# A two-layer graph network on one core: bf16 pieces by TensorE, later zero fills, words moved into layer 0, and another order of layer 1's tiles

## What is computed

```
h = relu(layernorm(x))
x = x + relu(h @ W_self + mean over edges(h[src]) @ W_neigh + b)           # layer 0
h = relu(layernorm(x))
e = sigmoid(relu([h[src], h[dst]] @ We1 + be1) @ We2 + be2)                 # one gate per edge
m = e * h[src];  messages = [max over edges(m), sum over edges(m)]
x = x + relu([messages, h] @ Wn1 + bn1) @ Wn2 + bn2 + h                     # layer 1
```

## Time and profile before

| | |
|---|---|
| median of 3 runs | 5438.78 us (5437.1 to 5440.79) |
| the profiled execution | 5435.6 us, span of its instructions 5433.9 us |
| busy DVE, POOL, ACT, PE | 4035.2, 3687.3, 2774.4, 2013.7 us |
| search | 0 to 179 us |
| sorting, ranks, words | 179 to 455 us |
| layer 0 | 455 to 2170 us |
| the rest of the early gathers | to 2435 us |
| layer 1 | 2435 to 5296 us |
| output scatters | to 5434 us |

### The profile page before, as it was taken

The page is one execution under the profiler, slowest core; times in us unless marked ns, Lnnn a source line. Parts: engine busy times, 40 slices in busy tenths (PEclk is TensorE's granted clock), DMA queues, the critical chain, the costliest instruction groups (busy, mean ns, idle before and its releaser), DMA issues.

```text
span 5433.9 us, 105141 instructions
## 1 busy us (share of the span) xinstructions
PE 2013.7 (37%) x18241; PEld 1777.4 (33%) x18241; DVE 4035.2 (74%) x8508; ACT 2774.4 (51%) x7285; POOL 3687.3 (68%) x3830
## 2 busy tenths in 40 slices
PE   0005899999999998000111111111111111111110
PEld 0004888888888888000000000101011111111110
DVE  6788788888888886006777778878888888887770
ACT  7304777887888886003444444444445444544440
POOL 5545216777777777767777777777777777766547
PEclk9999999999999999555555555555555555555555
DMA  7610315555555555554434444444444444443440
GB/s 212 166 24 27 41 52 173 160 160 158 163 160 160 158 163 167 158 156 101 124 113 124 124 122 125 124 133 126 132 133 135 133 142 136 142 134 118 123 98 24
DMA packets 491280, 696.11 MB, mean 128 GB/s; under 512 B 249885, under 2 KB 339843, under 8 KB 491163
## 3 DMA queue, kind: packets, MB, share of 16 engines
q0 software_dynamic: 181472, 381.28, 26.1%
q1 hardware_dynamic: 228085, 172.05, 10.3%
q10 hardware_dynamic: 81638, 141.95, 7.8%
HBM read 513.68 MB, written 163.18 MB: 125 GB/s over the span
## 4 chain that ended last, share of the span: by engine, by line
PE 22%; issue 20%; POOL 19%; DVE 17%; DMA 8%; ACT 7%; ACTq 4%; DVEq 3%; POOLq 0%; SPq 0%
POOL counts_f L580 13%; PE ps_acc L1867 10%; PE ps L1859 9%; DMA counts_f<-early_rows 5%; POOL extra_f L580 4%; DVE act_w L1450 4%; ACT counts_f L1627 3%; DMA counts_f<-hA_table,stage 2%; DVE pre L1444 2%; DVE run_max L1467 2%; ACT msg L1726 1%; DVE z L1456 1%; POOL out_dram L727 1%; ACTq L1726 1%; DVE pre L1059 1%
## 5 line engine op out<-in xcount | busy, mean ns | idle before, releaser
L580 POOL DMA_INDIRECT counts_f<-hA_table,stage x2144 | 2070.9, 966 | 794.3 <-issue 632.1
L1627 ACT ACTIVATE counts_f<-ps 128x784 bf16<-128x784 f32 x1568 | 1269.3, 823 | 468.6 <-PE ps L1859 385.7
L1444 DVE TENSOR_TENSOR pre<-counts_f,ps 128x512 f32 (+1 forms) x862 | 588.6, 683 | 825.2 <-SPq L897 316.9
L580 POOL DMA_INDIRECT extra_f<-hA_table,estage x984 | 932.1, 947 | 314.4 <-issue 290.4
L1726 ACT ACTIVATE msg<-counts_f,gate (+1 forms) x3448 | 921.5, 337 | 315.9 <-ACT gate L1721 293.8
L1867 PE MATMUL ps_acc<-pieces_f,counts_f 128*128 128x192 bf16 x9604 | 1021.3, 247 | 2.4 <-issue 2.4
L1867 PEld LDWEIGHTS ps_acc<-pieces_f,counts_f 128*128 128x128 bf16 x9604 | 885.7, 138 | 3.3 <-issue 2.8
L1859 PE MATMUL ps<-hot 128*128 128x196 bf16 x6272 | 820.6, 253 | 127.0 <-ACT counts_f L1627 106.5
L1938 PE MATMUL ps_acc<-ident,h_tile 128*64 128x128 f32 x98 | 38.6, 394 | 2210.3 <-DVE cat L1503 2210.3
L1721 ACT ACTIVATE gate<-z,be_col (+1 forms) x862 | 256.2, 297 | 1165.1 <-DVE z L1456 820.5
L1938 PEld LDWEIGHTS ps_acc<-ident,h_tile 128*64 128x64 f32 x98 | 12.6, 129 | 2226.4 <-issue 2226.4
(11 more groups left out here) (231 smaller groups left out, 2853.5 us busy)
## 6 DMA issues: line engine op xcount, KB each, us to landing
early_rows<-extra_f SPq DMA_DIRECT2D x294, 384.0 KB
counts_f<-early_rows ACTq DMA_DIRECT2D x98, 1152.0 KB
counts_f<-hA_table,stage POOLq DMA_INDIRECT x2144
counts_f<-counts_f SPq DMA_DIRECT2D x67, 288.0 KB
extra_f<-hA_table,estage POOLq DMA_INDIRECT x984
own<-own_rows ACTq DMA_DIRECT2D x98, 130.0 KB
hA_table<-node ACTq DMA_DIRECT2D x98, 96.0 KB
ranked_rows<-zeros SPq DMA_DIRECT2D x1, 3724.0 KB, 50.4
```

Source lines behind the costliest of these rows:

```text
L580: return pool.indirect_dma_start(to, None, table, bass.IndirectOffsetOnAxis(ap=idx, axis=axis))
L1444: v.tensor_tensor(pre[:, :, :], rows[:, :, D:WROW], ps_b[:, bass.ds(i & 1, 1), :].to_broadcast([P, SLOTS, H]), ALU.add).then_inc(s_pre, 1)
L1627: act.activation(counts[:, c, nodes, :].rearrange("p (b h) t -> p b (h t)", h=2), ps_pairs[g & 1][:, :].rearrange("p (b w) -> p b w", b=BA ...
```

## The change

1. ACT's wait for its input goes into the loop of the search. The first search step counts a pair of columns, then takes the rows of that pair, and stages them, instead of waiting for all ten columns first.
2. The two zero fills are issued after the twelfth of the fourteen sorted stores.
3. The second and third pieces are made by PE and ACT in 14 groups of 7 tiles: PE puts features minus first piece (identity and negative identity) in PSUM, ACT copies it to bf16; then the same with both pieces taken off. POOL's four subtractions and ACT's two large copies go. The negative identity `minus_b` is a new constant.
4. The sum over 64 bins becomes six additions that halve the array.
5. The words for degrees over 64 (`node_deg`) are made right after `s_thr`; the others (`late_words`) between phase(3, 1) and phase(4, 0) of layer 0, and a new semaphore `s_places` holds back POOL (before the early gathers), SP (before the loads of late rows) and ACT (before layer 1).
6. A tile of rank t goes to place min(2t, 2T-1-2t): heaviest, lightest, second heaviest, second lightest and so on. `tile_rank` is made to fit (8 small instructions for one), and two instructions move each node's place.

```diff
-            pool.wait_ge(s_first, 2 * TITER)
-            for h in range(2):
-                half = slice(h * (T // 2), (h + 1) * (T // 2))
-                pool.tensor_tensor(x_nodes[:, half, :], h_nodes[:, half, :], pieces[:, half, 0:D], ALU.subtract
-                                   ).then_inc(s_rest, 1)
...
-                pool.tensor_tensor(pieces[:, half, 2 * D:3 * D], x_nodes[:, half, :], pieces[:, half, D:2 * D],
-                                   ALU.subtract).then_inc(s_piece, 1)
...
             pool.wait_ge(s_row, 16)
+            pool.wait_ge(s_places, 1)
...
-            sp.wait_ge(s_start, 1)
+            with in_one_block(sp, 0, TITER - 1) as it:
+                store_sorted(it)
             sp.dma_start(extra_rows.rearrange("(t p) d -> p t d", p=P),
...
             sp.dma_start(ranked_rows.rearrange("(t p) w -> p t w", p=P),
...
+            store_sorted(TITER - 1)
...
             sp.wait_ge(s_recw, 16 * T)
+            sp.wait_ge(s_places, 1)
...
+            st.link(v.tensor_scalar(tile_rank[:, :], half_f, -2.0, float(T - 1), ALU.mult, ALU.add))
+            st.link(v.scalar_tensor_tensor(out=tile_rank[:, :], in0=tile_rank[:, :], scalar=odd_f, in1=half_f,
+                                           op0=ALU.mult, op1=ALU.add))
+            st.done(v.tensor_scalar(tile_rank[:, :], tile_rank[:, :], float(P), 1.0, ALU.mult, ALU.add))
...
-            search_step(0)
+            for a in range(PARTS):
+                at = slice(PASS + a * PCOLS, PASS + (a + 1) * PCOLS)
+                count(0, a)
+                rows_of(at, PASS + (a + 1) * PCOLS)
+                stage_rows(at, a)
...
+            rounded_up(node_deg[:, :], RUN, crow[:, 2, :], 1)
+            st.link(v.tensor_scalar(crow[:, 2, :], crow[:, 2, :], -1.0, 1.0, ALU.add, ALU.max))
+            word_sums(crow[:, 2, :], 8)
...
-            v.wait_ge(s_piece, 2)
+            v.wait_ge(s_piece, 2 * TITER)
...
-            st.link(v.tensor_reduce(cols2[:, :], order.rearrange("p b t -> p t b"), AX.X, ALU.add))
+            half = BINS // 2
+            while half > 1:
+                at = order_flat[:, 0:half * T]
+                st.link(v.tensor_tensor(at, at, order_flat[:, half * T:2 * half * T], ALU.add))
+                half //= 2
+            st.link(v.tensor_tensor(cols2[:, :], order_flat[:, 0:T], order_flat[:, T:2 * T], ALU.add))
...
+            st.link(v.tensor_scalar(cols[:, :], cols3[:, :], -2.0, float(2 * T - 1), ALU.mult, ALU.add))
+            st.link(v.scalar_tensor_tensor(out=cols3[:, :], in0=cols3[:, :], scalar=2.0, in1=cols[:, :],
+                                           op0=ALU.mult, op1=ALU.min))
...
+            phase(3, 0)
+            phase(3, 1)
+            late_words()
+            phase(4, 0)
+            phase(4, 1)
...
-            act.wait_ge(s_q, 2)
             with in_one_block(act, 0, SITER) as it:
+                act.wait_ge(s_q, 2)
...
+            def second(g):
+                act.wait_ge(s_rest, max(1, 2 * g))
+                act.activation(tiles_of(g, 1), rest_in(g), ACT.Copy).then_inc(s_sec, 1)
...
+            act.wait_ge(s_places, 1)
...
+            def rest(g):
...
+                pe.matmul(bank, ident[:, :], h_nodes[:, at, :].rearrange("p t d -> p (t d)"), start=True, stop=False)
+                pe.matmul(bank, minus_b[:, :], pieces[:, at, 0:D], start=False, stop=True).then_inc(s_rest, 1)
```

More of the change, by code:

```diff
@@ L404, in gnn_kernel @@
         s_ctl = sem("s_ctl")
+        s_places = sem("s_places")
         s_tidx = sem("s_tidx")
@@ L749, in _, with store_sorted @@
             sp.dma_start(flat_src[E:E + SRC_PAD].unsqueeze(0), src_tail[0:1, :]).then_inc(s_tab, 16)
-            sp.wait_ge(s_start, 1)
+            sorted_by_tile = sorted_rows.rearrange("(t p) w -> p t w", p=P)
+            def store_sorted(it):
+                for h in range(2):
+                    wait_alone(sp, s_srt, 4 * it + 2 * h + 2)
+                    tiles_at = bass.ds(it * (2 * THALF) + h * THALF, THALF)
+                    sp.dma_start(sorted_by_tile[:, tiles_at, :], rows_sb[:, tiles_at, :]).then_inc(s_srtw[h], 16)
+            with in_one_block(sp, 0, TITER - 1) as it:
+                store_sorted(it)
             sp.dma_start(extra_rows.rearrange("(t p) d -> p t d", p=P),
@@ L1361, in _ @@
             phase(2, 1)
-            for q in range(3, 5):
-                phase(q, 0)
-                phase(q, 1)
+            phase(3, 0)
[3 more added lines that the diff above has]
+            phase(4, 1)
             first = st.now()
@@ L1612, in _, with rest_in, tiles_of, third @@
                 act.dma_start(h0_by_tile[:, tiles_at, :], h_nodes[:, tiles_at, :]).then_inc(s_h0w, 16)
-            for h in range(2):
-                half = slice(h * (T // 2), (h + 1) * (T // 2))
-                act.wait_ge(s_rest, h + 1)
-                act.activation(pieces[:, half, D:2 * D], x_nodes[:, half, :], ACT.Copy).then_inc(s_sec, 1)
+            def rest_in(g):
+                return ps_4[:, (g & 1) * BANK:(g & 1) * BANK + THALF * D].rearrange("p (t d) -> p t d", d=D)
+            def tiles_of(g, k):
+                return pieces[:, g * THALF:(g + 1) * THALF, k * D:(k + 1) * D]
+            def second(g):
+                act.wait_ge(s_rest, max(1, 2 * g))
+                act.activation(tiles_of(g, 1), rest_in(g), ACT.Copy).then_inc(s_sec, 1)
+            def third(g):
+                act.wait_ge(s_rest, min(2 * g + 3, 4 * TITER))
+                act.activation(tiles_of(g, 2), rest_in(g), ACT.Copy).then_inc(s_piece, 1)
+            second(0)
+            for g in range(1, 2 * TITER):
+                second(g)
+                third(g - 1)
+            third(2 * TITER - 1)
             act.wait_ge(s_w, W_DMAS)
@@ L1833, in _, with rest_of_rest @@
             pe.matmul(ps_y[:, 2 * D:2 * D + 1], ones[0:1, 0:P], thr[0:1, 0:1], start=True, stop=True).then_inc(s_thrb, 1)
+            def rest(g):
+                if g >= 2:
+                    pe.wait_ge(s_piece, g - 1)
+                bank = ps_4[:, (g & 1) * BANK:(g & 1) * BANK + THALF * D]
+                at = slice(g * THALF, (g + 1) * THALF)
+                pe.matmul(bank, ident[:, :], h_nodes[:, at, :].rearrange("p t d -> p (t d)"), start=True, stop=False)
+                pe.matmul(bank, minus_b[:, :], pieces[:, at, 0:D], start=False, stop=True).then_inc(s_rest, 1)
+            def rest_of_rest(g):
+                pe.wait_ge(s_sec, g + 1)
+                bank = ps_4[:, (g & 1) * BANK:(g & 1) * BANK + THALF * D]
+                at = slice(g * THALF, (g + 1) * THALF)
+                pe.matmul(bank, ident[:, :], h_nodes[:, at, :].rearrange("p t d -> p (t d)"), start=True, stop=False)
+                pe.matmul(bank, minus_b[:, :], pieces[:, at, 0:D], start=False, stop=False)
+                pe.matmul(bank, minus_b[:, :], pieces[:, at, D:2 * D], start=False, stop=True).then_inc(s_rest, 1)
+            pe.wait_ge(s_first, 2 * TITER)
+            rest(0)
+            for g in range(1, 2 * TITER):
+                rest(g)
+                rest_of_rest(g - 1)
+            rest_of_rest(2 * TITER - 1)
             pe.wait_ge(s_bins, 1)
```

91 lines of the change are left out of this document (48 added, 43 removed).

## The result

The changed kernel takes **5262.13 us** (median of 4 runs, 5257.23 to 5262.5), the kernel before 5437.94 beside it on the same chip; the ratio is **0.9675 (95%: 0.9659 to 0.9692)**. Forecast were 5268, between 5238 and 5325. The profiled execution took 5262.5 (span 5260.8), 173.1 us of span less than before.

A forecast was written before the change was run, and what follows sets the result against it. Layer 1 was taken as bound by POOL in heavy tiles and DVE's early-row loads in light ones, the front by DVE. 48.4 us ahead plus 121 in layer 1, 169 off 5435.6, plus 3.2 gave 5268, range 5238 to 5325.

The forecast's parts named there:

- What bounds layer 1: Layer 1: POOL bounds the heavy tiles; in light ones POOL waits for DVE, held by early-row loads 24.4 us apart.
- the 121: Layer 1: with tiles alternated POOL never waits, so its gathers take 2722 us instead of 2843, 121 less.
- Search: Search ahead of layer 0: ACT's wait inside its loop and counts first save 9 us, bounds 0 and 10.
- Zero fills: Sort stage: without early fills, 3 us less at the run gathers and 3 at DVE's loop entry, -6.
- Pieces: Ahead of layer 0: DVE's 25.05 us instruction falls to 0.63 once POOL's subtractions are gone, -24.4 us.
- Sum over bins: Ahead of layer 0: six additions replace the 11.85 us sum over bins, two added instructions cost 0.5; -4.2 us.
- Words: 13.8 us leave the path ahead of layer 0; 36 instructions inside it cost PE 9; net -4.8.
- Scatters and what lies behind: After layer 1's gathers: the 98 scatters go on at 1.29 us and end with the span, unchanged.
- (a): Layer 1: ring too small or early loads later, only part of the stalls go; gain 50 there, 5341; chance 8%.
- (b): Layer 1: alternation does nothing, each tile still goes by its slower engine; only 48 us gained, 5391; chance 4%.
- (c): Ahead of and in layer 0: loop-entry gaps stay, PE loses 12; 33 of 48 us left, 5285; chance 8%.
- (d): Layer 1: POOL's gathers stretch beside busier DVE; gain gone at 0.079 us more each, 5512 at mean 1.08; chance 2%.

The follow-up runs named there:

- e9: e1 with one more DVE maximum (128x1024 fp32, about 1.2 us) in each layer 1 tile but the first and last: 5411.06 us, ratio 0.9956.
- e1: The changed kernel with layer 1's tiles back in order of load, all else kept: 5384.18 us, ratio 0.9903.
- e2: The kernel before with only the alternating order of tiles added: 5309.78 us, ratio 0.9772.
- e7: The changed kernel with ACT's wait for the nodes' ids ahead of its search loop again: 5267.91 us, ratio 0.9687.
- e6: The changed kernel with the two zero fills issued early again, at s_start, ahead of the sorted stores: 5266.47 us, ratio 0.9682.
- e3: The changed kernel with the pieces made as before, by POOL's four subtractions and ACT's two large copies, without PE: 5288.9 us, ratio 0.9729.
- e4: The changed kernel with the late words in one block ahead of layer 0, right before s_ctl: 5264.85 us, ratio 0.9682.
- e10: The changed kernel with layer 1's messages in PSUM instead of SBUF: 5232.23 us, ratio 0.9623.

## Why the prediction was right, step by step

**What bounds layer 1.** Right. POOL bounded it wherever it didn't wait, the light tiles went by their load's round, and DVE was the bound of neither half: e9 shows that 1.2 us more of it per tile don't lengthen a light tile. The pace of 1.27 us a gather, on which the 121 stood, measured 1.269 (2720.0 us for 2143 steps). Measured gain 123.1, and 122 to 125 in e1 and e2. Of the 123, 113 are POOL's long gaps and 10 are gathers less often stretched (mean 966 before, 961 after); the prediction had no term for the second. Two small slips in its working: light tiles have up to 9 chunks, by its own 21 columns, where it says 8; and its range doesn't follow from the cases named for it. A pace of 1.255 with the words free gives about 5228, not 5238, and a gain of 90 with 30 ahead gives 5319, not 5325. The result lies within either.

**Search** (-9): measured -7.4 at `s_start`, of which the wait's place 6.4 (e7, 177.81 against 171.36). The step that was too large: the third pass was taken to come in time at once, but the first counts now wait for their gathered rows.

**Zero fills** (-6): the two gaps gave 3.45 and 3.2, together 6.7; e6 brings 7.25 back.

**Pieces** (-24.4): measured -24.4 between the old and the new timeline, and +24.4 in e3.

**Sum over bins** (-4.2): measured -3.8.

**Words** (13.8 saved, 9 lost, net -4.8): `s_ctl` came 13.6 earlier through them (what the other four items leave of 55.9), and layer 0 grew by 7.3 to 7.7 us: its first hot row came 56.7 earlier, its last product with the pieces 49.4 earlier, layer 1's first gather 49.0. That is net 5.9 to 6.3 for 4.8; the 9 taken for PE's loss was too high. The split needs a word: what pays are the 10 instructions that went into the wait for run gathers (4 us). The 36 inside layer 0 gain nothing (e4).

**Scatters and what lies behind.** As forecast, they only shifted: 98 of them from 5123.01 on, 1.30 us apart, as before.

**The rivals.** (a) and (b) didn't happen: POOL's waits for ACT are 22.8 + 13.2 us in their two largest rows. (c) didn't either. (d) is the one to look at again. Its 2% were fair for its size, since it needed 0.079 us more per gather and the change brought none (966 before, 961 after). But its mechanism was at work in both kernels, at 0.019 us a gather before and 0.014 after (against the 947 of e10), and the prediction's reading of it, "in these rows the pace didn't fall where DVE was at 0.80", looked at the busy share where the kind of instruction decides. A mean of 966 over a usual 945 was in the earlier trace rows and could have been asked about: 30 us lay in it. The forecast came out all the same, because this hold was already in the 1.27 that it took from the rows.

## What to carry to other kernels

Where two engines take turns at being late over a stream of uneven items, interleave light and heavy ones before making either engine faster; a short period that doesn't change with one engine's load belongs to a transfer's round. If GpSimd issues indirect transfers at a steady pace, sort its durations by what VectorE was doing when they began; an operand moved from SBUF to PSUM can be worth more than an instruction removed. Work that must go into a busy pipeline goes in single instructions, not in a block, and a block cost the same inside as ahead here.

## What I had not expected of the hardware

- The hold between DVE and GpSimd is exact to some 20 ns. A gather (945 ns alone) that begins beside a DVE maximum or sum of two SBUF operands ends 0.82 us behind it; beside an fp32 copy within SBUF 0.81 us behind it, and one already running ends 0.12 us behind it. In the other direction GpSimd's subtractions held DVE's `valid` for 25 us.
- The copy of 128x2048 fp32 takes 1.32 us, a maximum of half the elements 1.21.
- TensorE's granted clock, and what its column says where there is no record. The pieces gave PE a first burst of work from 217 to 260; the changed kernel's trace has the clock at its lower level (1.2 GHz) from 263 to 427, past the start of layer 0. The kernel before shows 1.00 in the same stretch. Stretches of the changed kernel, then of the kernel before:

```profile
265.00:400.00 135.00, 1.49 (x5) 1.01 (x5) 116.78 (x580) 0.00 (x0) 34.30 (x37) 0.50 0.40 74
403.00:413.00 10.00, 5.41 (x30) 3.28 (x30) 8.14 (x6) 4.61 (x6) 7.56 (x9) 0.50 0.15 44
413.00:435.00 22.00, 19.96 (x162) 15.78 (x161) 15.78 (x15) 17.37 (x22) 16.82 (x18) 0.68 0.10 29
```
```profile
265.00:400.00 135.00, 0.00 (x0) 0.00 (x0) 116.71 (x626) 5.63 (x2) 64.94 (x48) 1.00 0.12 26
```

```profile
470.94 1.54 PE L1859 MATMUL ps<-hot 128*128 128x196 bf16 x8 [0.37 <-ACT counts_f L1627]
472.84 0.51 PE L1859 MATMUL ps<-hot 128*128 128x196 bf16 x4 [0.36 <-ACT counts_f L1627]
```
```profile
412.37 1.53 PE L1926 MATMUL ps<-hot 128*128 128x196 bf16 x8 [0.38 <-ACT counts_f L1668]
```

  So layer 0 began at the lower level in both kernels. It left that level 12 us after its first hot row before the change and 23 us after it in the changed kernel. The burst isn't the reason, since e3, which has none, needs 23 us too (427.95 to 450.7); the reason stays open. It cost little: the first two steps of layer 0 take 64.2 us together, as before.
- The entry of DVE's sort loop costs 3.45 us without any releaser (3.1 to 3.6 in the ten other kernels with late fills), and the gap grows to 6.6 while large fills occupy the queues (e6).
- Layer 0 varies: with the same code in it, its first hot row and layer 1's first gather lie 1993.4 to 2000.0 us apart over nine kernels. Differences under 7 us behind layer 0 say nothing by themselves.
